# Recurrence of a gated linear-attention layer: the transpose of the layernorm rows behind the output matmuls

## What is computed

```python
q = hidden_states @ Wq                                # k and v the same way
beta = jax.nn.sigmoid(hidden_states @ Wb + bb)
q = silu(causal_dwconv(q, qconv_w, qconv_b))          # 4 taps over the tokens, k the same way
q = layernorm(q.reshape(Bs, Ls, H, DK), qn_w, qn_b)   # over the 128 of a head, k the same way

def step(S, inp):
    q_t, k_t, v_t, b_t = inp
    b = b_t[..., None, None]
    S = (1.0 - b) * S + b * (v_t[..., :, None] * k_t[..., None, :])
    o_t = jnp.einsum('bhvk,bhk->bhv', S, q_t)
    return (S, o_t)
_, os = lax.scan(step, S0, (qs, ks_, vs, bs))
```

## Time and profile before

| | us |
|---|---|
| median of three runs | 2605.1 (2599.21 to 2606.36) |
| the profiled execution's own time | 2600.33 |
| its span, from the first instruction to the last | 2598.5 |
| TensorE busy in it | 2456.1 (95%) |
| VectorE busy | 1904.5 (73%) |
| ScalarE busy | 1241.8 (48%) |
| GpSimd busy | 849.1 (33%) |
| mean granted TensorE clock | 0.977 of full speed |

### The profile page before, as it was taken

The page is one execution under the profiler, slowest core; times in us unless marked ns, Lnnn a source line. Parts: engine busy times, 40 slices in busy tenths (PEclk is TensorE's granted clock), DMA queues, the critical chain, the costliest instruction groups (busy, mean ns, idle before and its releaser), DMA issues. The chain is left out here.

```text
span 2598.5 us, 43686 instructions
## 1 busy us (share of the span) xinstructions
PE 2456.1 (95%) x14784; PEld 2175.3 (84%) x14784; DVE 1904.5 (73%) x3396; ACT 1241.8 (48%) x2025; POOL 849.1 (33%) x442
## 2 busy tenths in 40 slices
PE   4889989989999999999999999996999998999997
PEld 4778878889999989999989999996788887888886
DVE  5589999989999999999999999998422123432232
ACT  5455455545555656555555555554533223322221
POOL 1245544433434343443434343444000000221220
PEclk9999999999999999999999999998999999999999
DMA  7566566576655675666676656664551102431320
GB/s 283 166 212 212 194 221 221 201 263 205 215 195 211 210 274 195 211 218 205 210 249 231 200 204 210 211 208 142 180 204 49 65 32 73 151 121 45 113 90 23
DMA packets 242375, 462.74 MB, mean 178 GB/s; under 512 B 59382, under 2 KB 162038, under 8 KB 221178
## 3 DMA queue, kind: packets, MB, share of 16 engines
q10 hardware_dynamic: 107648, 244.34, 27.3%
q1 hardware_dynamic: 125946, 192.21, 22.0%
q0 software_dynamic: 8704, 25.19, 3.1%
HBM read 371.99 MB, written 98.07 MB: 181 GB/s over the span
## 5 line engine op out<-in xcount | busy, mean ns | idle before, releaser
L1023 DVE SCALAR_TENSOR_TENSOR xn_rows<-ps_proj,conv,xn_rows 128x1021 f32<-128x1021 f32 x381 | 486.8, 1278 | 11.6 <-ACT xn_rows L900 2.5
L1221 PE MATMUL ps_proj<-xt_hi,w_hi 128*128 128x512 f32 x1008 | 409.0, 406 | 20.1 <-DMA xt_lo<-scratch_xt_lo 12.0
L1223 PE MATMUL ps_proj<-xt_hi,w_lo 128*128 128x512 f32 x1008 | 398.5, 395 | 0.0
L1222 PE MATMUL ps_proj<-xt_lo,w_hi 128*128 128x512 f32 x1008 | 397.1, 394 | 0.0
L784 POOL TENSOR_TENSOR rc_k_state<-rc_tok_k,k_norm_rows 128x1024 f32<-128x1024 f32 x64 | 153.6, 2400 | 599.6 <-DVE rc_q_silu L1035 511.9
L1243 PE MATMUL ps_proj<-wv_hi,xt_hi 128*128 128x256 f32 x1024 | 295.2, 288 | 0.7 <-PEq L75 0.7
L1244 PE MATMUL ps_proj<-wv_lo,xt_hi 128*128 128x256 f32 x1024 | 289.8, 283 | 0.0
L1245 PE MATMUL ps_proj<-wv_hi,xt_lo 128*128 128x256 f32 x1024 | 289.8, 283 | 0.0
L1221 PEld LDWEIGHTS ps_proj<-xt_hi,w_hi 128*128 128x128 f32 x1008 | 191.9, 190 | 59.1 <-DMA xt_lo<-scratch_xt_lo 13.3
L1653 DVE TENSOR_TENSOR ff_wide_lo<-ff_wide,ff_wide_hi 128x512 fp32r<-128x512 f32 x64 | 44.4, 693 | 248.7 <-ACT ff_wide_hi L1568 248.7
L1223 PEld LDWEIGHTS ps_proj<-xt_hi,w_lo 128*128 128x128 f32 x1008 | 191.4, 190 | 42.0
(11 more groups left out here) (181 smaller groups left out, 5757.0 us busy)
## 6 DMA issues: line engine op xcount, KB each, us to landing
rc_q_rows<-scratch_rows ACTq DMA_DIRECT2D x64, 1024.0 KB, 5.1
rc_k_rows<-scratch_rows ACTq DMA_DIRECT2D x64, 1024.0 KB, 4.6
rc_decay_all<-scratch_decay ACTq DMA_DIRECT2D x64, 512.0 KB, 5.4
rc_cum_all<-scratch_cum ACTq DMA_DIRECT2D x64, 512.0 KB, 3.7
scratch_o<-rc_o_sb ACTq DMA_DIRECT2D x64, 512.0 KB, 3.5
w_hi<-scratch_w_split SPq DMA_DIRECT2D x48, 512.0 KB, 4.7
w_lo<-scratch_w_split SPq DMA_DIRECT2D x48, 512.0 KB, 5.5
wv_hi<-scratch_wv_split SPq DMA_DIRECT2D x24, 512.0 KB, 3.9
```

The lines of the kernel that those rows point to most:

```text
L1023: nc.vector.scalar_tensor_tensor(out=act_cm[j][:, back:], in0=projected[:, 0:L - back], scalar=conv[par][:, j, t:t + 1], in1=act_cm[j][:, ...
L1221: nc.tensor.matmul(out, hi, xt_hi[:, k, cols], start=k == 0, stop=False)
L1222: nc.tensor.matmul(out, hi, xt_lo[:, k, cols], start=False, stop=False)
L1223: last = nc.tensor.matmul(out, lo, xt_hi[:, k, cols], start=False, stop=k == KC - 1)
```

## The change

On TensorE, in `step`, the block that transposes the roots and shifts of head B stands behind the block of head D's outputs instead of in front of it. Nothing else differs; its waits and its semaphore are the same, and the other engines' programs are unchanged.

```diff
                 if A_.live:
                     project_v(0)
                     project_v(1)
-                if B_.live:
-
-                    after_step(pe, "rstd_done", B_.i)
-                    after_step(pe, "shift_done", B_.i)
-                    if D_.live:
-                        after_step(pe, "scores_done", D_.i)
-                    nc.tensor.transpose(work(par, SC)[0:4 * NC, 0:P], rstd_shift[:].rearrange("p j k c -> p (j k c)"),
-                                        ident[:]).then_inc(S["rows_turned"], 1)
                 if D_.live:
 
                     after_step(pe, "states_done", D_.i, NC - 1)
...
                     last.then_inc(S["outputs_mm"], 1)
+                if B_.live:
+
+                    after_step(pe, "rstd_done", B_.i)
+                    after_step(pe, "shift_done", B_.i)
+                    if D_.live:
+                        after_step(pe, "scores_done", D_.i)
+                    nc.tensor.transpose(work(par, SC)[0:4 * NC, 0:P], rstd_shift[:].rearrange("p j k c -> p (j k c)"),
+                                        ident[:]).then_inc(S["rows_turned"], 1)
```

## The result

The changed kernel takes 2710.67 us (median of four runs, 2709.61 to 2712.32) where the kernel before takes 2604.01 on the same chip: a ratio of 1.0413, 95% interval 1.0395 to 1.0431, or 107 us. The forecast was 2692 us, 2655 to 2740. The profiled execution has a span of 2707.8 us, 109.2 more than before.

A forecast was written before the change was run, and what follows sets the result against it. The prediction took TensorE, busy 95% of the span, to bound the kernel. Its terms 76 + 2 + 8 + 5 = 91 us on the profiled 2600.3 gave 2691.3, forecast as 2692 us, range 2655 to 2740.

The forecast's parts named there:

- What decides: Later steps: q's silu, queued behind ScalarE's row copy, ends 3.3 us later with only 1.76 or 1.31 us to spare.
- The even stretch: Recurrence, 560 to 1740 us: TensorE waits for q's silu in 45 steps, 23 x 1.6 + 22 x 1.8 = 76 us.
- The other kind: Even-stretch steps whose row store is slow, 1.31 us to spare: 1.8 us each in 22 steps, between 1.6 and 2.4.
- the slow store would meet less traffic: Even stretch: issued 3.3 us later, the 3.5 us row store may land faster, making its steps cost 1.6 us too.
- VectorE is covered: Even stretch: q's rows arrive 7.0 us after the transpose, about when the turn runs; VectorE's 24.5 us fit into 26.9.
- The sign I gave for the case that the store decides: VectorE's waits for q's rows longer than those of the turn would show that the store, not the silu, decides.
- The first sequence: Six steps with waits of about 4 us lose 1.3 us each, short-wait steps nothing: 8 us, ends 3 and 15.
- Changes of sequence and the end: Three changes of sequence hide the late silu, 2 us in all; behind the last transpose the delay shows fully, 5 us.
- The clock falls in the new waits: Rival: new TensorE waits lower its clock; every step 2773 us (0.06), under half of them 2710 to 2740 (0.10).
- ScalarE's gaps close: Rival: the later start overlaps ScalarE's idle gaps before the silu and behind the row copy; 2620 to 2629 us, chance 0.05.
- Faster: Rival: outputs fill TensorE's 28.1 us of waits for the shifts in the first sequence; 2572 us, chance 0.03.
- No change: Rival: the chain behind the row copy doesn't reach the turn because ScalarE's queue isn't kept in order; 2600 us, chance 0.03.

The follow-up runs named there:

- e1: Changed kernel, with ScalarE computing the next head's q silu before the copy of the transposed rows instead of behind the outputs' copy: 2662.67 us.
- e10: Changed kernel, with VectorE's scale and shift of q reading a constant tile instead of q's rows (output not the layer's): 2680.41 us.
- e2: Kernel before, with only ScalarE's q silu moved ahead of the row copy, the transpose still in front of the outputs: 2604.52 us.
- e3: Kernel before, with the transpose behind the outputs in the first sequence's 16 steps only: 2626.27 us.
- e11: Kernel before, with VectorE's scale and shift of q reading a constant tile instead of q's rows (output not the layer's): 2588.69 us.

## Why the prediction was right, and where its terms were off

**What decides.** Right. TensorE never waited at the transpose; ScalarE's queue behind the row copy did the damage. In the odd steps the chain from the transpose to the silu's end kept its length (7.1 to 7.2 us), the turn gained about the waits foretold (47, 74.4 us, against some 45 and 70 to 85), and e1 takes those waits away. The 3.3 us of delay less 1.76 of spare time, 1.6, is nearly what the odd steps pay, 1.65, with a little luck: the wait at the turn is 1.4 to 1.5 us in most of them, and the other 0.2 us no wait names.

**The even stretch**, forecast 76, measured 88.2 us (in e10, with the rows out of the way, 90.1). The odd steps were 1.65 against 1.6. The other kind, put at 1.8, is the mis-sized term: it cost 2.4 on the mean over 21 steps, 50 us. In four of them (29.05 us three times and 29.58 once, against a median of 27.21) the clock fell, which is 8 us; without these the mean is 2.0. The guess that the slow store would meet less traffic was right: in the step shown it took 2.2 us instead of 3.5, and the copy of the outputs starts 4.3 us after the transpose in 19 of the 21 steps, as in the odd ones, where it had started 4.7 us or more behind it. What these steps pay beyond the odd ones lies behind that copy: ScalarE's gap before the silu is 0.85 us in one and 1.15 in the next, against 0.76, and the turn starts 0.25 us after the silu's end instead of 0.05. So eleven of these steps wait 1.7 us and seven 2.0, where I had read one kind. DMA issues, after, 943 to 955 us:

```profile
scratch_rows<-rc_row_parts ACTq DMA_DIRECT2D x1, 16.0 KB, 2.2
```

The 0.11 us between small matmuls follows from 30 outputs in some 3.4 us, not from the two starts named beside it.

**"VectorE is covered"** was right for the time and wrong as a statement. VectorE waits 74.3 us for q's rows, which I had put at 7.0 us after the transpose; in the step shown VectorE gets them 8.09 us after it, with 1.46 us idle:

```profile
951.34 1.23 DVE L1033 TENSOR_TENSOR rc_q_silu<-rc_q_silu,rc_q_rows 128x1024 f32<-128x1024 f32 x1 [1.46 <-DMA rc_q_rows<-scratch_rows]
```

In the later sequences e10 shows that those waits add nothing, but only because TensorE is already held longer by the silu. With the silu away the rows cost 34 us (e1 against e2). The sign I gave for the case that the store decides, VectorE's waits longer than the turn's, was no sign at all: the two rows read 74.3 and 74.4.

**The first sequence** is the step that failed: forecast 8 us (ends 3 and 15), measured 20.7 between transposes 2 and 14, and 22 for the whole of e3. I had priced the steps that begin behind a long wait at 1.3 us, and those that begin behind a short one at "nothing", because the delay "finds TensorE with a 4 us wait ahead". It came out the other way round: the six steps of the second kind grew by 3.1 us each on the mean, 18.6 in all, and the first kind cost 2.1 us together. One step priced at nothing, after the change, from the timeline:

```profile
373.91 0.27 PE L1317 MATMUL rc_ps_work<-ident,rc_rstd_shift 128*32 128x128 f32 x1
...
382.88 1.23 DVE L1033 TENSOR_TENSOR rc_q_silu<-rc_q_silu,rc_q_rows 128x1024 f32<-128x1024 f32 x1 [0.86 <-DMA rc_q_rows<-scratch_rows]
...
400.30 1.22 DVE L1116 TENSOR_TENSOR rc_scores<-rc_ps_work,rc_dmat 128x1024 f32<-128x1024 f32 x1
...
401.66 1.19 PE L1306 MATMUL rc_ps_work<-rc_v_beta,rc_scores 128*128 128x128 f32 x4 [3.77 <-DVE rc_scores L1116]
...
407.79 0.27 PE L1317 MATMUL rc_ps_work<-ident,rc_rstd_shift 128*32 128x128 f32 x1
```

Here VectorE is the engine that sets the pace: from 382.88 on it works without a wait for rows or for TensorE until the scores. In two steps together its work is the same before and after, 55.9 us, and only its idle time grows, from 2.3 to 5.5 us (windows of before, then of after, two steps each; the third busy time is VectorE's):

```profile
329.33:387.50 58.17, 53.10 (x346) 48.26 (x347) 55.85 (x93) 32.27 (x53) 28.11 (x12) 0.97 0.63 208
...
373.91:435.34 61.43, 54.42 (x349) 49.09 (x346) 55.89 (x93) 31.86 (x53) 28.12 (x12) 0.94 0.61 197
```

Behind the scores the outputs run for 6.13 us, after a wait of 3.77 us, with a granted clock of 0.53 (windows of after, 401.6 to 407.7 us, columns as in the earlier trace rows),

```profile
401.60:407.70 6.10, 6.04 (x30) 6.07 (x31) 6.00 (x5) 0.00 (x0) 0.00 (x0) 0.53 1.04 311
```

and then the rows take 8.97 us to VectorE: 33.88 us from transpose to transpose. Before, the outputs ran beside VectorE's work; now they stand in the loop transpose, rows, VectorE, scores, outputs, transpose, at half the clock (what the clock's share of the cost is was not tried). Four of the six steps of this kind grew from about 30 to 33.8 us, and their neighbours stayed at about 28. With the rows out of the loop the cost is 3.4 us (e10 - e11), with them 26.2 (e1 - e2). So the wait that I had taken for cover was VectorE's own lateness, to which a later transpose adds.

**Changes of sequence and the end**, forecast 2 and 5 us: the two later changes cost nothing (29.61 and 29.69 us before, 29.76 and 29.66 after), the first was 4.2 us shorter. The end, counted with the block of outputs that is now in front of the third transpose (+3.8) and missing behind the last (-2.4), cost 1.4: q's rows arrived 6.9 us behind the last transpose instead of 8.5, and paid half of the delay back.

So the sum had 91 us for 109: the two mis-sized terms, +12 and +13, and +3 from a part that the change doesn't touch, are partly undone by -6 and -4 in the small ones.

**The rivals.** *The clock falls in the new waits*: in 4 of 45 steps, 8 us, where I had priced 18 to 48 for that rival. That the time fell on its lower end, 2710, is mostly the two mis-sized terms' doing, of which the clock is 8 us. Windows of after: behind two of those waits, 2.00 us long, and, in the last row, around a wait of 2.00 us (it ended at 1336.21) that left the clock alone:

```profile
895.00:899.00 4.00, 3.96 (x15) 3.44 (x16) 3.45 (x8) 3.89 (x4) 0.82 (x1) 0.57 0.33 91
1115.90:1120.90 5.00, 4.93 (x19) 4.11 (x20) 4.44 (x11) 4.24 (x4) 1.81 (x1) 0.66 0.43 120
...
1334.00:1340.00 6.00, 4.00 (x22) 3.33 (x22) 4.54 (x9) 4.97 (x5) 0.83 (x1) 1.00 0.55 183
```

The Trainium skill ("TensorE: Matmul & The Clock Gate", section "HAM oscillation — how this bites in real kernels") describes a kernel in which a wait in every tile lowers the clock in every tile. The waits there are for a DMA and some 3 to 5 us long, longer than those at the turn, so I was wrong to read 2773 us from it; the trace shows 45 steps with a wait of 0.8 to 2.6 us each, and a granted clock that stayed at 1.00 in 41 of them. *ScalarE's gaps close*: they didn't, 0.85 us in front of the silu as before. *Faster*: the outputs did wait for the scores, 27.6 us. *No change*: the chain reaches the turn.

## What to carry to other kernels

A small instruction on an engine that never waits can still be the start of a loop over other engines: add up from it, along every in-order queue and every transfer behind it, until it comes back to the same instruction, and compare with the step. Do this for each loop, since the slower hides the next (here 88 us hid 34), and taking away the wait that the profile names gives back only the difference. Where an engine already waits, ask whose lateness it is before calling it cover: if it is that of the loop that is being lengthened, the wait grows instead of absorbing.

## What the runs showed that was not expected

The clock's answer to waits of equal length differs: seven waits of TensorE at the turn were 2.00 us long, and behind three of them (ending at 895.04, 1115.97 and 1226.09) the granted clock fell to 1.2 GHz, behind four (786.49, 1336.21, 1555.94, 1664.47) it stayed at 2.4. A wait of 2.55 us that ended at 677.89 left it at 2.4, one of 2.55 that ended at 1827.38 didn't. Behind the shorter waits, 0.8 to 1.7 us, it never fell.

The kernel before gained 15.6 us when VectorE didn't wait for q's rows (e11), where its waits for them in the first sequence add up to 6.7. In the two profiled executions, which differ by 11.7 us, the gain lies in the first sequence (4.7 us), at the first change of sequence (5.8) and in small parts elsewhere, none in the later steps (25.29 us). Why the change of sequence is shorter was not tried further.
